# Last pass of a gated cross-attention and mixture-of-experts kernel: the gated product is turned through memory and by VectorE

## The reference, cut to what matters

```python
x = x + tanh(g_xattn) * scan(...)                      # x1, 4096 tokens x 1024
n = layernorm(x)
out = moe(n)            # 4 rows of the experts' results for each token, weighted
shared = silu(n @ shared_gate) * (n @ shared_up) @ shared_down     # inner width 1024
x = x + tanh(g_ffn) * (out + shared)
```

## Time and profile before

| | |
|---|---|
| median of 3 runs | 4038.11 us (4036.43 to 4038.69) |
| profiled execution, its own time | 4033.5 us |
| span of the profile | 4031.7 us |
| last pass, first matmul to end of the span | 3479.39 to 4031.7 us |
| PE busy in the last pass, 3615 to 3915 us | 100% |

### The profile page before, as it was taken

How to read it: one execution, slowest core, us unless ns; L and a number is a source line. 1 busy time by engine, 2 the same in 40 slices (tenths; PEclk the granted TensorE clock), 3 DMA queues, 4 the chain that set the end, 5 groups by cost and what they waited for, 6 DMA issues and landing times. The chain is left out here.

```text
span 4031.7 us, 58882 instructions
## 1 busy us (share of the span) xinstructions
PE 3681.9 (91%) x20528; PEld 3051.6 (76%) x20528; DVE 3111.3 (77%) x3712; ACT 2114.9 (52%) x2610; POOL 2008.3 (50%) x1201
## 2 busy tenths in 40 slices
PE   8898498888888888869999979999999999999999
PEld 3444388888878888758887868888888888788887
DVE  7899899999999999978888866666666666455555
ACT  3678699889989989821111134444444444200000
POOL 0233199999999999923333333333333333122222
PEclk9999599999999999979999989999999999999999
DMA  7677853653553553377766667777777777677543
GB/s 235 242 280 277 288 166 101 167 163 111 151 174 116 147 168 120 99 235 218 225 215 211 225 209 255 249 251 250 248 253 248 250 252 250 224 281 257 196 161 120
DMA packets 374393, 835.44 MB, mean 207 GB/s; under 512 B 96656, under 2 KB 155792, under 8 KB 364880
## 3 DMA queue, kind: packets, MB, share of 16 engines
q1 hardware_dynamic: 339264, 765.97, 56.3%
q0 software_dynamic: 34816, 67.24, 5.8%
q10 hardware_dynamic: 144, 0.00, 0.0%
HBM read 619.21 MB, written 245.27 MB: 214 GB/s over the span
## 5 line engine op out<-in xcount | busy, mean ns | idle before, releaser
L1125 POOL TENSOR_TENSOR h<-h,c 128x1024 f32<-128x1024 f32 x512 | 1206.4, 2417 | 24.4 <-DVE h L1108 21.5
L1108 DVE TENSOR_TENSOR_SCAN h<-da,dbu 128x1024 f32<-128x1024 f32 x512 | 1135.2, 2273 | 47.1 <-ACT dbu L1070 27.9
L1078 ACT ACTIVATE da<-dl,ad 128x1024 f32<-128x1024 f32 x512 | 584.2, 1141 | 100.3 <-DVE h L1108 88.9
L1157 PE MATMUL psy<-ident,h 128*128 128x128 f32 x4096 | 562.1, 281 | 81.6 <-POOL h L1125 60.6
L1903 POOL DMA_INDIRECT xg<-scratch_xn,ids x256 | 328.9, 1285 | 597.9 <-DVE xT_place L2190 520.1
L1070 ACT ACTIVATE dbu<-psb 128x512 f32<-128x512 f32 x1020 | 548.0, 589 | 30.7 <-PE psb L1147 27.9
L1157 PEld LDWEIGHTS psy<-ident,h 128*128 128x128 f32 x4096 | 444.9, 142 | 129.6 <-POOL h L1125 91.2
L2195 DVE TENSOR_TENSOR wsp<-arena,wsp 128x2048 fp32r<-128x2048 f32 x146 | 329.7, 2287 | 91.9 <-ACT wsp L2140 91.8
L1147 PE MATMUL psb<-m,du_taps 128*128 128x128 f32 x2048 | 294.6, 291 | 43.6 <-ACT dbu L1070 35.1
L1147 PEld LDWEIGHTS psb<-m,du_taps 128*128 128x128 f32 x2048 | 259.3, 193 | 79.5 <-ACT dbu L1070 73.0
L1451 POOL DMA_INDIRECT scratch_tab<-tok_s,si_s x128 | 132.1, 1032 | 358.8 <-DVE si_s L1819 327.4
(11 more groups left out here) (244 smaller groups left out, 8667.2 us busy)
## 6 DMA issues: line engine op xcount, KB each, us to landing
arena<-in_w SPq DMA_DIRECT2D x192, 1024.0 KB, 7.0
du_taps<-scratch_duT SPq DMA_DIRECT2D x496, 128.0 KB, 2.9
c<-scratch_c SPq DMA_DIRECT2D x64, 512.0 KB, 13.0
scratch_xT<-xT_s SPq DMA_DIRECT2D x32, 1024.0 KB
scratch_ob<-ob SPq DMA_DIRECT2D x64, 512.0 KB, 2.6
xT_place<-scratch_xT SPq DMA_DIRECT2D x32, 1024.0 KB, 4.9
scratch_duT<-duT SPq DMA_DIRECT2D x52, 512.0 KB, 4.0
xz<-in_x SPq DMA_DIRECT2D x32, 512.0 KB, 5.5
```

The source lines that it names most:

```text
L1078: act.activation(da[k % 2][:, :], dl[:, i % 2, :], ACT.Exp, scale=ad[:, i % 2, n:n + 1]).then_inc(s_da, 1)
L1108: dve.tensor_tensor_scan(h[:, k % HR, :], da[k % 2][:, :], dbu[:, (k // GN) % 2, k % GN, :], 0.0, ALU.mult, ALU.add).then_inc(s_scan, 1)
L1125: pool.tensor_tensor(h[:, k % HR, :], h[:, k % HR, :], c[:, n, :], ALU.mult).then_inc(s_hc, 1)
L1157: mm = pe.matmul(psy[:, t, :], h[:, k % HR, t * P:(t + 1) * P], ident[:], is_transpose=True, start=(n == 0 and t % 4 == 0), stop=(n == NST ...
```

## The change

In the last pass alone:

- `multiply` and `Silu` write the gated product `sg` in another column order. Each block of 128 columns is cut into four parts of 32, and all first parts come first, then all second parts, and so on.
- ScalarE, which before issued no transfer in this pass, issues the store of `sg` to a new scratch tensor (256 KB, `store_hidden`) behind the multiply. In the next turn, in front of `h_head`, it waits for that store to land and issues four loads of a quarter (64 KB each, in runs of 128 float32, `load_hidden`) into the new tile `hq`.
- VectorE transposes the 32x32 blocks of `hq` in place (`h_blocks`, 128x512). ScalarE's head and VectorE's rest read `hq` through a strided view in place of `psH`.
- TensorE's four transposes of each turn and the tile `psH` are gone.
- VectorE's order was finish(t-2), h_rest(t-1), multiply(t). It is now h_blocks(t-1), h_rest(t-1), finish(t-2), multiply(t). In `finish` the half comes ahead of the four sums, but for the last tile, where it stays behind them.

```diff
+            hq = sb("hq", [P, HB])
+            gated_hidden = sg[:].rearrange("p (q j c) -> p j q c", q=NQ, c=QB)
+            gate_product, up_product = (v[:].rearrange("p (j q c) -> p j q c", q=NQ, c=QB) for v in (psG, psU))
+            hidden_blocks = hq[:].rearrange("p (g j c) -> p j g c", g=NQ, c=QB)
...
         def _(pe):
-                    if not route and not first:
-                        h_transpose(t - 1)
...
         def _(act):
+                    if not route and not first:
+                        load_hidden(t - 1)
                     if not first:
                         h_head(t - 1)
...
+                    act.activation(gated_hidden, gate_product, ACT.Silu).then_inc(s_sg, 1)
+                    if not route:
+                        store_hidden(t)
...
+            def store_hidden(t):
+                act.wait_ge(s_h, t + 1)
+                act.dma_start(dr["h"][t], sg[:]).then_inc(s_hst, 16)
+
+            def load_hidden(t):
+                act.wait_ge(s_hst, t * 16 + 16)
+                after(act, s_hlo, t)
+                for q in range(NQ):
+                    act.dma_start(hq[q * QB:(q + 1) * QB, :].rearrange("p (g c) -> p g c", g=NQ),
+                                  dr["h"][t][:, q * P:(q + 1) * P].rearrange("(g p) c -> p g c", g=NQ)).then_inc(s_hq, 16)
...
         def _(dve):
+            def h_blocks(t):
+                dve.wait_ge(s_hq, (t + 1) * 16 * NQ)
+                dve.transpose(hq[:], hq[:]).then_inc(s_htr, 1)
...
             def finish(t, j, par):
+                def half():
+                    dve.wait_ge(s_d, t + 1)
+                    dve.scalar_tensor_tensor(out=x1t[:, par, :], in0=psO[:], scalar=gate[:, 0:1], in1=x1t[:, par, :],
+                                             op0=ALU.mult, op1=ALU.add).then_inc(s_half, 1)
+                last = isinstance(t, int) and t == TT - 1
                 dve.wait_ge(s_acl[par], j * 32 + 32)
+                if not last:
+                    half()
...
+                    if not route and not first:
+                        h_blocks(t - 1)
+                    if not first:
+                        h_rest(t - 1)
                     if not route and not second:
                         finish(t - 2, j - 1, par)
-                    if not first:
-                        h_rest(t - 1)
...
             if not route:
                 finish(TT - 2, TT // 2 - 1, 0)
+            if not route:
+                h_blocks(TT - 1)
             h_rest(TT - 1)
```

More of the change, by code:

```diff
@@ L1207, in shared_pass @@
         rows = lambda m, part, half: matrix(m, part)[:, halves[half]].rearrange("p (k f) -> p k f", f=HB)
-        hidden = psU[:]
-        psO, psH = ps("psO", [P, H]), ps("psH", [P, KF, P])
+        psO = ps("psO", [P, H])
+        gated_hidden, gate_product, up_product = sg[:], psG[:], psU[:]
+        if not route:
[3 more added lines that the diff above has]
+            hidden_blocks = hq[:].rearrange("p (g j c) -> p j g c", g=NQ, c=QB)
         if route:
+            psH = ps("psH", [P, KF, P])
             psX = ps("psXT", [P, 2, 4, P])
@@ L1596, in _ @@
             turns(pe, TT // 2, pair, last=1)
-            h_transpose(TT - 1)
+            if route:
+                h_transpose(TT - 1)
             down(TT - 1)
@@ L1635, in pair @@
                     act.wait_ge(s_g, t + 1)
-                    after(act, s_htr, t)
-                    act.activation(sg[:], psG[:], ACT.Silu).then_inc(s_sg, 1)
+                    if route:
+                        after(act, s_htr, t)
+                    act.activation(gated_hidden, gate_product, ACT.Silu).then_inc(s_sg, 1)
+                    if not route:
+                        store_hidden(t)
                     if route and first:
@@ L1664, in h_head @@
                 after(act, s_d, t)
-                act.activation(hT[:, 0], psH[:], ACT.Copy).then_inc(s_hhi, 1)
+                if route:
+                    act.activation(hT[:, 0], psH[:], ACT.Copy).then_inc(s_hhi, 1)
+                else:
+                    act.activation(hT[:, 0].rearrange("p j (g c) -> p j g c", c=QB), hidden_blocks, ACT.Copy).then_inc(s_hhi, 1)
+            def store_hidden(t):
[7 more added lines that the diff above has]
+                                  dr["h"][t][:, q * P:(q + 1) * P].rearrange("(g p) c -> p g c", g=NQ)).then_inc(s_hq, 16)
             def scaled_out(t, j, par):
@@ L1688, in _ @@
                 scaled_out(TT - 2, TT // 2 - 1, 0)
+            if not route:
+                load_hidden(TT - 1)
             h_head(TT - 1)
@@ L1713, in h_rest @@
                 dve.wait_ge(s_hhi, t + 1)
-                dve.tensor_tensor(hT[:, 1], psH[:], f32(hT[:, 0]), ALU.subtract).then_inc(s_hlo, 1)
+                if route:
+                    dve.tensor_tensor(hT[:, 1], psH[:], f32(hT[:, 0]), ALU.subtract).then_inc(s_hlo, 1)
+                else:
+                    heads, rests = (hT[:, c].rearrange("p j (g c) -> p j g c", c=QB) for c in range(2))
+                    dve.tensor_tensor(rests, hidden_blocks, f32(heads), ALU.subtract).then_inc(s_hlo, 1)
+            def h_blocks(t):
+                dve.wait_ge(s_hq, (t + 1) * 16 * NQ)
+                dve.transpose(hq[:], hq[:]).then_inc(s_htr, 1)
             def multiply(t):
@@ L1729, in finish @@
                                              in1=ac[:, par, :], op0=ALU.mult, op1=ALU.add).then_inc(s_sum, 1)
-                dve.wait_ge(s_d, t + 1)
-                dve.scalar_tensor_tensor(out=x1t[:, par, :], in0=psO[:], scalar=gate[:, 0:1], in1=x1t[:, par, :],
-                                         op0=ALU.mult, op1=ALU.add).then_inc(s_half, 1)
+                if last:
+                    half()
                 dve.wait_ge(s_half, t + 1)
```

6 lines of the change are left out of this document (4 added, 2 removed).

## The result

The changed kernel takes 4291.61 us (median of 4 runs, 4290.66 to 4293.43), against 4037.45 us (4036.43 to 4038.69) for the kernel before. The ratio is 1.063, with an interval of 1.0611 to 1.0648. The direction is as forecast, and the size is far outside the range: I gave 4118, with 4180 as the upper end. Even the contention rival, at 4196, falls short by 96 us.

What follows compares the result with a forecast made beforehand. The prediction took DVE's closed loop through memory and `finish` to replace PE as bound, its terms summing to 19.4 us a turn against 16.79. Thirty turns gave 78 us, the tail 2: 4038.1 + 80 = 4118 us, range 4050 to 4180.

Steps and rivals of the forecast that it cites:

- contention rival: Last pass: quarters take turns with SP's 2 MB and land after it, 22.0 us a turn, 4196 us; chance 0.14.
- The bound and the mechanism: Last pass: DVE's closed loop of round trip and `finish` takes over from PE as bound, 19.4 us a turn.
- the landing of the last quarter: Loop term on ACT's queue, from the last quarter's issue until it lands: 3.1 us, between 2.3 and 5.
- high end: Loop with the long terms, 5.1 for the store and 5 for the quarter's landing: 22.6 us a turn.
- the store: Loop term on ACT, from the store of `sg` until the next issue may go: 3.8 us, ends 2.1 and 7.9.
- The issues: Loop term on ACT: four issues of the quarters, the last starting 1.57 us after the first.
- the blocks: Loop term on DVE: `h_blocks`, transposing the blocks of `hq`, takes 0.71 us for 512 elements.
- have more than a turn: Last pass: the gathers start behind the sums and have more than a turn, so they are not late.
- The first two turns don't change by more than a microsecond: Start of the last pass: the first two turns have no `finish`, so they change by at most a microsecond.
- PE's pause: Last pass: PE idles about 3 us a turn in front of the down product, and its clock may fall.
- The tail: Behind the last multiply, tile 31: 27 us against 24.5, so 2 to 3 us more.
- The low end: Loop with 2.1 for the store and 2.3 for the quarter's landing: 16.9 us a turn.

Runs made afterwards that it cites:

- e2: The changed kernel with `finish` put ahead of `h_blocks` again on VectorE: 4062.27 us, ratio 1.0074 to the kernel before.
- e8: The changed kernel's memory route with VectorE's whole order of before (`finish` first, half behind the sums): 4067.12 us, ratio 1.0089 to the kernel before.
- e4: The changed kernel without the gathers of the last pass, so the output lacks the experts' part: 4201.69 us in one run.
- e9: Changed kernel, VectorE's old order, SP's loads held from the second tile until the quarters landed, tile 1's gathers held for tile 0's quarters: 4056.91 us, ratio 1.0052.
- e10: The changed kernel with SP's loads held from the third tile until the quarters landed and the gathers left out: 4042.72 us in one run.
- e11: The changed kernel with VectorE's order of before and the gathers left out, so the output lacks the experts' part: 4034.60 us in one run.
- e7: The changed kernel with one contiguous read-back load in 2 KB pieces instead of four quarters, output's last part wrong: 4185.35 us in one run.
- e3: The changed kernel with SP holding `ac`, `x1t` and transposed tokens from the third tile until the quarters landed: 4132.17 us in one run.
- e5: The changed kernel with the store in 512-byte pieces by four issues and the read-back as one load in 2 KB pieces: 4263.06 us in one run.

## Why the prediction was right in direction and wrong in size

- **The bound and the mechanism** were right. DVE's loop with the round trip and `finish` in one line sets the turn, DVE waits for the quarters and not for PE, and PE pauses in front of the down product with the half as the releaser. The experiments show that it takes both: the order alone costs 0.2%, the route alone 0.7 to 0.9% (e2, e8), both together 6.3%.
- **The step that failed** is the landing of the last quarter, "I take 3.1", with a high end of 5. It measured 11.7 early and 7.7 late (issues at 4201.81, transpose at 4210.88), and 9.4 in the mean of the 30 turns. The 6.3 us above 3.1 are 190 us in the 30 turns, less 27 for the store, which came out 0.9 below my 3.8. The issues (1.7 in the mean) and the blocks shift it by 3 us each, one up and one down. That is the difference of 163 between 240.8 and my 78. What took the place of the 3.1 are two things that the runs show: the traffic of both other streams beside the quarters (11.7 with both, 7.4 to 7.5 with one, 1.95 with none), and, inside it, 3.5 to 4.0 us early in the pass before the first piece even starts.
- **Why the high end was too low.** I priced the quarters against 2 MB of SP's loads alone, and had put the gathers aside with "have more than a turn". That asks whether the gathers are late, not whom they delay. They are another 2 MB, issued from 3621.06 to 3624.97, just as the quarters go. And I had the quarters land when SP's 4.8 us are through, as if the sum of bytes were all.
- **How the queues share.** Counting the data packets in the trace by their end, from 3632 to 3635 us, gives 28 to 36 pieces in each us on each of the three queues, 31 in the mean: 8 KB on SP's, 4 KB on POOL's, 512 bytes on ACT's. So 31 x 12.5 KB is the 395 GB/s of the windows, and ACT's share of it is 4%. The records show the order too. When a queue is alone, a record starts 3 to 4 ns before the end of another. In seven such stretches of the changed kernel with all three queues at work, 705 of 716 pieces of POOL end so on a start of SP, 646 of 751 of SP on one of ACT, and 657 of 716 of ACT on one of POOL, while the queue's own next piece starts there no oftener than at other distances (by chance some 25 at each). Each DMA engine takes one piece of each queue in turn. At this pace the 512 pieces of the four quarters need over 16 us. About half of them were left when the others were nearly through at 3635, and went in 1.2 us. The contention rival named the mechanism, and its size had the same gap.
- **A slip in the sum:** the high end of 22.6 takes 5.1 for the store, while the term itself gives 7.9. With 7.9 it would be 25.4, near the measured 24.8, but by luck, since the store took 2.9.
- The Trainium skill, page "DMA: Bandwidth & Descriptors", section "Queues, rings and completion order", says that an engine goes round between the queues packet by packet, and gives 9 to 17 descriptors as typical for a packet. The round is as the trace shows it. But here the queues alternate at the level of single pieces, as the count above shows, and the measurement decides.
- **"The first two turns don't change by more than a microsecond"** was wrong: +11.8 us. I looked only for `finish` in them. The down product of tile 0 was not waiting for memory before, and now waits for a store and a load in the busiest moment of the pass, with the first gathers. With these left out or held it is 13.2 to 14.8 (e4, e9, e10, e11).
- **The store** was 2.8 to 3.0 in the loop, not 3.8. In the closed loop it is issued when the engines are idle. The stores in the earlier trace rows were not.
- **PE's pause** was to be 3 us, and is up to 9.2, since it is what the loop leaves over PE's work. The clock fell as said.
- **The tail** was to cost 2 to 3, and cost 1.8. The blocks, head and rest (0.71, 0.63, 0.69) and the half ahead of the sums were right to a tenth of a us.
- **The low end** of my sum, 16.9, is what e10 measures (16.95), with the streams away. In part that is luck: the store took 2.78, not 2.1, the landing 1.95, not 2.3, and the issues 1.33, not 1.57. But each term was right to 0.7 us for DMA engines that are idle, and under load another price was needed. The same holds for the 2.6 and 2.15 us that the prediction works out by the formula of the Trainium skill, page "DMA: Bandwidth & Descriptors", section "Anatomy of one DMA", where the fit is given for transfers that GpSimd issues.

Could the route pay at all? The gain is bounded by 30 x 0.47 = 14 us, and e2 and e8 reach it in their last turns. In an early turn of the kernel before, the DMA engines are busy for 0.74 x 16.79 = 12.4 us, which leaves 4.4. The quiet round trip of e10 needs 2.78 + 1.33 + 1.95 = 6.1. So in the first half of the pass the round trip has to share the engines with something. In e9 that cost PE next to nothing on the side of the round trip, and the held tokens cost the 16.9 us. To hold `ac` and `x1t` alone and issue the tokens ahead of them was not tried, so it is open how much of the loss can be had back early in the pass. Late, with 0.49, 8.6 us are free, and there it fits. To turn only the late tiles through memory could bring at most about 13 x 0.47 = 6 us before the tail, which is under the 0.2% that can be told here. I didn't run it, and this last step is argued, not shown.

## What to carry to other kernels

Before a short transfer is put into a dependent chain, list all that is issued from 3 us before it until it should land, on every queue. The time when all of that is through is the price for a transfer in small pieces (the quarters: 13.3 us). With larger pieces it can land earlier (e7: 8.7 us). A count of its own bytes, or the landing time of its neighbours in a quiet stretch, gives only the low end. If it must go beside others, its pieces should be as large as theirs. Whoever holds back other transfers for its sake has to look at who waits for them: in e9 that was PE. And a wait on memory goes to the end of an engine's turn, behind the work that doesn't need it: here the order of two calls was worth 225 us.

## What the runs showed of the hardware that I had not expected

- Three DMA queues with work moved equal numbers of pieces, whatever their size: about 31 per us each, of 8 KB, 4 KB and 512 bytes, one piece of each in turn. A load of 256 KB in 512 pieces took 13.3 us from its first issue beside the other two streams. With either one left its last part landed 7.4 to 7.5 us after the last issue, with none 1.95.
- The first piece of a load of ACT started 0.96 us behind its issue when the other queues were quiet (e10), in early turns of the loop 2.6 to 3.4 beside one of the streams (e3, e4) and 3.2 to 4.0 beside both, in 512 pieces or in 128 (the changed kernel and e7). The cause is open.
- Four times larger pieces took the load from 13.3 to 8.7 us, not to a quarter. Smaller pieces on the store's side took the store from 3.0 to 8.5 (e5).
- The same 256 KB store needed 2.8 to 3.0 us on idle engines, 8.2 to 9.1 in the midst of loads and gathers (e9, e2), and 9.6 in the first turn.
